# A Flamingo block on one core: the same steps of a hand-ordered pipeline in another order

## The chip, the cores and the metric

The kernel runs on one core of one Trainium2 chip. The metric is the device time of one execution in microseconds. Three runs of the kernel before gave 1331.11, 1333.94 and 1334.88 us; the median is 1333.94 us.

## The reference

The inputs are `x` (32 x 256 x 256, float32), a context `ctx_1024` (32 x 77 x 256), two gates and the weights. Cut to what matters:

```python
# cross attention, 8 heads of 128, no softmax over keys: everything is linear in the keys
f_q, f_k, f_v = proj(layernorm(x)), proj(ctx), proj(ctx)     # LN, then @ w_in.T, 8 heads
cosine_sim    = f_q @ f_k.T / (|f_q| |f_k|)
mixed         = cw*cosine_sim + vw*cosine_sim*decorr + ww*(q_ratio x k_ratio)   # weights per head
x = x + tanh(g_xattn) * ((mixed @ f_v) @ w_out.T + b_out)
# second attention, 16 heads of 16, softmax over 256 positions
z = layernorm(x); q, k, v = z@Wq, z@Wk, z@Wv
z = softmax(k q^T / 16, over the queries)^T @ v
z = gelu(l2norm(l2norm(z @ Wo) @ Wff))
x = x + tanh(g_ffn) * z
```

## The kernel before, in words

A setup phase (to about 170 us of the profile) computes statistics that need all of `x` and the whole context. Then `main_phase` works through 16 pairs of two batch rows each. The work on a pair is cut into some 260 named steps. Each step belongs to one engine and a few instructions:

- TensorE: `fk0..2` (keys of the heads), `G0..5` and `V0..5` (keys times the in- and out-projection), `zT0/1` and `zz0/1` (transposes), `q0..7` (queries, for their norms alone), `d0..5` (scores), `a0` (transpose of the query factors), `y0/1` (output of the first attention), `pq`, `pk`, `pv` (second attention's projections), `S0..15` (its scores), `P0..7` (probabilities times v), `O0..3` (output and the two l2 norms).
- ScalarE: a step with `.h` copies a bank of PSUM to its float16 high half; `X0..31` are the exponentials, `E0..3` copy the attended values, `O0.`..`O3.` take the squares, `F3` is the gelu, `pv0.v`, `a0.v` copy.
- VectorE: a step with `.l` subtracts the high half from the same bank and frees the bank; `M0..31` are the maxima of the scores, `R0..7` scale v, `d0.o`, `y0.o`, `q0.o` empty their banks, `z` normalises the rows of `x` for the next pair but one, `ln1/ln2` are the second layer norm, `qs1/qs2` the query factors, `F2/F4` the end of a pair.
- GpSimd: `rk`, `m0.l..m5.l`, `qpow`, `lpow`, `F1` (powers).
- SyncE issues every DMA: `ldx` (512 KB of `x` into `xin`, read by `z`), `aux`, `sqe0/sqe1` (12 broadcasts into `sqE`, read by `d0.o`, `d1.o`), `vt0/vt1` (DMA transposes, read by `y0`), `wq`, `ldy` (512 KB into `x2S`, read by `y0.o`), `res` (`x2S` to `x2`), `parts0/1` (queries and keys of the second attention to DRAM), `back0..3` (from there into `qstack` and `kstack`, read by `S0`, `S4`, `S8`, `S12`), `out`.

One list, `ORDER`, holds all steps. `run` lets each engine walk the list and execute its own steps, so the list fixes each engine's queue and nothing else; semaphores do the rest. A step never starts before its predecessor on its engine, and two steps of different engines are tied only by a semaphore. The list is software-pipelined: `lead(step)` says to which of three pairs in flight a step of one turn belongs (0, 1 or 2 turns back), and `MOVED` holds the exceptions. `HEAD` and `TAIL` are the shortened lists for the first and last two turns; 14 turns of `ORDER` lie between them.

All matmul steps but `S`, `P` share `WORK` = 3 banks of PSUM in the order of the list:

```python
CHUNKS = [s for s in ORDER if any(t.startswith(s + ".") for t in ORDER)]
A_INDEX = {name: k for k, name in enumerate(CHUNKS)}
...
def wait_free(eng, name, pair):
    eng.wait_ge(drained[A_INDEX[name] % WORK], uses(name, pair))
```

So a chunk can't start until the chunk three places before it in the list has been emptied (its `.l`, `.o` or `.v` step). There are 46 chunks, so at the turn of the list, where the last chunk and the first one both have bank 0, `a0` waits for the chunk right before it, `pv0`. Lines that the rows below name: L894 to L896 are the three products of every split matmul, L1388 `a0`, L1436 `S`, L1447 `P`, L1506 every `.h`, L1519 `pv.v`, L1533 `X`, L1557 `F3`, L1633 `a0.l`, L1684 `d.o`, L1693 `y.o`, L1730 `M`, L1602 `F1`, L1292 `parts`, L1302 `back`, L1245 `ldx`, L1250 `ldy`.

Of the kernel before, what the change touches and what calls it, by code (L numbers as in the profile page):

```python
# [974 lines left out]
TAIL = """
G4.h M2 a0 a0.v pv1 G4.l G5 a0.h M3 a0.l G0 aux X2 G5.h G5.l pv1.v G0.h S2 M4 V5 M5 G1 G0.l X3 G2 V5.h X4 res V5.l V2
S3 G1.h R0 back1 sqe0 G1.l G2.h V2.h M6 V4 V2.l M7 X5 S4 X6 M8 G2.l V4.h X7 M9 P0 X8 S5 V4.l d0 M10 X9 R1 M11 S6 X10
P1 sqe1 X11 d0.o d1 E0 M12 S7 vt0 M13 m0.h d1.o R2 d2 m0.l vt1 X12 X13 m1.h d2.o M14 M15 d3 m2.h d4 S8 wq m1.l X14 L0
m2.l ldy d3.o d4.o X15 P2 R3 m3.h d5 M16 m4.h X16 back3 S9 P3 M17 y0 M18 X17 m3.l S10 d5.o m5.h M19 X18 m4.l y0.o X19
M20 M21 X20 S11 X21 E1 m5.l M22 R4 M23 y1 L1 X22 S12 y1.o M24 P4 X23 M25 ln1 X24 R5 S13 O0 M26 O0. X25 M27 X26 S14 P5  # L980
lpow X27 M28 E2 S15 ln2 X28 M29 zz0 R6 L2 zz0.h zz1 zz1.h M30 zz0.l X29 zz1.l M31 X30 X31 O1 R7 P6 pq0 pq0.h pq0.l pk0
P7 pk0.h pk0.l E3 parts0 L3 O2 O1. O3 O2. pk1 O3. back0 F1 pq1 S0 pk1.h pk1.l pq1.h F2 pq1.l F3 M0 S1 back2 parts1 X0
M1 pv0 X1 pv0.v +back1 F4 +M2 out +M3 +S2 +X2 +M4 +pv1 +M5 +X3 +back3 +pv1.v +X4 +X5 +S3 +M6 +X6 +R0 +M7 +P0 +S4 +M8
+X7 +S5 +M9 +R1 +X8 +X9 +M10 +M11 +X10 +S6 +X11 +M12 +P1 +M13 +S7 +R2 +X12 +E0 +X13 +S8 +M14 +M15 +L0 +X14 +P2 +M16
+X15 +M17 +R3 +S9 +X16 +X17 +M18 +M19 +X18 +X19 +P3 +S10 +S11 +M20 +M21 +E1 +R4 +M22 +X20 +L1 +X21 +X22 +P4 +M23 +S12
+X23 +S13 +M24 +X24 +M25 +M26 +R5 +X25 +M27 +X26 +S14 +P5 +M28 +X27 +X28 +E2 +M29 +S15 +M30 +X29 +L2 +M31 +X30 +X31
+O0 +R6 +O0. +O1 +P6 +R7 +P7 +E3 +L3 +O2 +O1. +O3 +res +O2. +O3. +F1 +F2 +F3 +F4 +out
""".split()
# [815 lines left out]
```

## Time and profile before

| | |
|---|---|
| median of three runs | 1333.94 us (1331.11 to 1334.88) |
| the profiled execution | 1326.34 us, span 1324.6 us |
| mean granted TensorE clock | 0.978 of full |
| TensorE, VectorE, ScalarE, GpSimd busy | 1174.8, 1086.3, 1011.5, 299.3 us |
| DMA packets' share of 16 engines | 47.4% |

The profile is of one execution, 8 us shorter than the median of the runs. Busy time is the time in which an engine works on an instruction; where one engine is named behind an arrow, its instruction ended the idle time before the row's own. Times in rows are microseconds from the start of the span.

### The profile page before, as it was taken

What the parts mean: (1) busy time and instruction counts of PE and PEld (TensorE: products, weight loads), DVE (VectorE), ACT (ScalarE), POOL (GpSimd) and SP (SyncE); (2) the same over time, 40 slices, a digit from 0 to 9 for tenths busy, and PEclk for the clock granted to TensorE, in tenths of its full rate; (3) what the DMA queues carried; (4) which work ended last, traced back from release to release, by engine and by line L of the source; (5) the groups of instructions that cost most, each with busy time, mean ns of one, the idle gap of its engine ahead of it and who ended that gap; (6) DMA issues with size and microseconds to landing.
All of it is one profiled execution on the core that took longest, in us unless ns stands there. A gap on an engine that the chain in (4) does not pass through costs nothing.

```text
span 1324.6 us, 34636 instructions
## 1 busy us (share of the span) xinstructions
PE 1174.8 (89%) x10322; PEld 746.5 (56%) x10322; DVE 1086.3 (82%) x3084; ACT 1011.5 (76%) x3333; POOL 299.3 (23%) x257
## 2 busy tenths in 40 slices
...
GB/s 259 139 164 20 3 38 96 114 142 110 160 86 183 63 205 51 216 42 202 58 205 42 217 42 216 52 199 69 193 76 180 89 169 99 159 110 149 106 160 17
DMA packets 247888, 162.30 MB, mean 123 GB/s; under 512 B 94538, under 2 KB 235559, under 8 KB 247848
## 3 DMA queue, kind: packets, MB, share of 16 engines
q1 hardware_dynamic: 247848, 161.80, 47.4%
...
## 4 chain that ended last, share of the span: by engine, by line
PE 39%; SPq 22%; issue 9%; ACT 6%; DMA 5%; DVE 5%; POOL 1%; ACTq 0%; POOLq 0%; DVEq 0%; PEldq 0%
PE work L894 11%; PE work L896 10%; SPq L1281 10%; PE work L895 10%; PE attended L1447 5%; DMA x2S<-in_x 4%; SPq L1273 3%; SPq L1302 2%; SPq L1292 2%; PE score L1436 1%; ACT zb L1557 1%; SPq L1262 1%; ACT L1557 1%; PE work L1344 1%; ACT prob L1533 1%
## 5 line engine op out<-in xcount | busy, mean ns | idle before, releaser
L1533 ACT ACTIVATE prob<-score,nm 128x256 f32<-128x256 f32 x1024 | 477.1, 492 | 52.1 <-DVE nm L1730 46.2
L1730 DVE TENSOR_REDUCE nm<-score 128x2 f32<-128x512 f32 x512 | 332.6, 680 | 20.7 <-PE score L1436 20.2
L1533 ACT ACTIVATION_READ_ACCUMULATOR prob<-score,nm 128x1 f32 x1024 | 229.4, 224 | 0.0
L1590 POOL TENSOR_TENSOR mTl<-md,mTh 128x512 f16<-128x512 f32 (+1 forms) x96 | 95.2, 1006 | 378.0 <-ACT mTh L1506 378.0
L1447 PE MATMUL attended<-prob,vsp 128*32 128x256 f32 x2048 | 134.4, 391 | 9.7 <-DVE vsp L1745 8.4
L1436 PE MATMUL score<-qstack,kstack 64*128 64x256 f16 x1024 | 92.6, 277 | 40.9 <-DMA kstack<-parts 27.1
L1648 DVE BATCH_NORM_STATS2 qst<-work 128x6 f32<-128x128 f32 x512 | 110.4, 282 | 15.3 <-PE work L896 15.3
L1602 POOL TENSOR_TENSOR nrs<-nrm,phalf 128x8 f32<-128x8 f32 x16 | 26.3, 1642 | 355.8 <-ACT zb L1553 355.8
L894 PE MATMUL work<-wTh,xTh 128*128 128x512 f16 x256 | 98.3, 384 | 4.2 <-DVE xTl L1642 3.0
L895 PE MATMUL work<-wTl,xTh 128*128 128x512 f16 x256 | 97.7, 382 | 0.0
L896 PE MATMUL work<-wTh,xTl 128*128 128x512 f16 x256 | 97.6, 381 | 0.0
L1447 PEld LDWEIGHTS attended<-prob,vsp 128*32 128x32 f32 x2048 | 56.2, 110 | 68.5 <-issue 25.2
L894 PE MATMUL work<-Vph,mTh 128*128 128x256 f16 (+1 forms) x320 | 87.4, 273 | 7.7 <-DVE x2S L1693 4.1
L1593 POOL TENSOR_TENSOR rq<-qft,mhalf 128x32 f32<-128x32 f32 x16 | 86.8, 5428 | 29.7 <-DVEq L1657 29.7
L894 PE MATMUL work<-xTh,Gh 128*128 128x256 f16 (+1 forms) x320 | 87.6, 274 | 3.2 <-DVE fkl L1639 1.7
L1684 DVE SCALAR_TENSOR_TENSOR md<-work,rkc,sqE 128x256 f32<-128x256 f32 (+1 forms) x160 | 69.5, 476 | 23.7 <-DMA sqE<-sq_rows 15.3
L895 PE MATMUL work<-xTl,Gh 128*128 128x256 f16 (+1 forms) x320 | 87.2, 273 | 0.0
L896 PE MATMUL work<-xTh,Gl 128*128 128x256 f16 (+1 forms) x320 | 87.2, 273 | 0.0
L896 PE MATMUL work<-Vph,mTl 128*128 128x256 f16 (+1 forms) x320 | 87.1, 272 | 0.0
L895 PE MATMUL work<-Vpl,mTh 128*128 128x256 f16 (+1 forms) x320 | 87.0, 272 | 0.0
L1436 PEld LDWEIGHTS score<-qstack,kstack 64*128 64x128 f16 x1024 | 33.0, 94 | 93.1 <-issue 39.7
L1551 ACT ACTIVATE junk<-work 128x256 bf16<-128x256 f32 x128 | 48.4, 389 | 39.0 <-PE work L896 37.7
...
## 6 DMA issues: line engine op xcount, KB each, us to landing
...
xin<-in_x SPq DMA_DIRECT2D x16, 512.0 KB, 8.6
x2S<-in_x SPq DMA_DIRECT2D x16, 512.0 KB, 4.1
...
```

What stands on the lines that cost most here:

```text
L894: nc.tensor.matmul(out, a["h"][at], b["h"][bt], start=first, stop=False)
L895: nc.tensor.matmul(out, a["h"][at], b["l"][bt], start=False, stop=False)
L896: return nc.tensor.matmul(out, a["l"][at], b["h"][bt], start=False, stop=last)
L1281: sp.dma_start_transpose(Vp[half][:, :, :, o * P:(o + 1) * P].rearrange("p b t o -> p (b t) o"), VT[half][:, o, :, :].rearrange("p b c -> ...
L1436: last = nc.tensor.matmul(sc[2 * i + e][:, jj * NQ:(jj + 1) * NQ], kstack[rows, j, b2 * NQ + k * P:b2 * NQ + (k + 1) * P], qstack[rows, j, ...
L1447: last = nc.tensor.matmul(pvb[32 * j:32 * j + 32, t, :], vsp[:, k, (4 * e + j) * 2 * FD:(4 * e + j + 1) * 2 * FD], prob[:, n % PG, e, j, : ...
L1533: nc.scalar.activation(prob[:, g % PG, e, j + jj, :], sc[n % SC][:, jj * NQ:(jj + 1) * NQ], ACT.Exp, bias=nm[:, u + jj:u + jj + 1], accum_ ...
L1590: nc.gpsimd.tensor_tensor(dst, src, emptied(e[:2], "h")[0], ALU.subtract).then_inc(m_ready, 1)
L1593: nc.gpsimd.tensor_tensor(rq[:], qft[:, 0, :, :], w["mhalf"][:].rearrange("p (t h) -> p t h", h=H), ALU.pow).then_inc(rq_ready, 1)
L1648: last = nc.vector.bn_stats(qst[:, t, 4 * half + h, :], bank(e)[:, h * DH:(h + 1) * DH])
L1684: last = nc.vector.scalar_tensor_tensor(md[0:r, c % 2, k * 2 * P:(k + 1) * 2 * P], bank(e)[0:r, k * 2 * P:(k + 1) * 2 * P], rkc[0:r, t, b2 ...
L1730: nc.vector.tensor_reduce(nm[:, u:u + 2], sc[n % SC][:, :].rearrange("p (u q) -> p u q", q=NQ), AX.X, ALU.max, negate=True).then_inc(max_r ...
```

## The change

`ORDER`, `HEAD` and `TAIL` are replaced by other permutations of the same steps, and `MOVED` by another table of leads. No instruction is added, removed or resized, and no semaphore or buffer changes; the waits are computed from the lists, as before.

```diff
 ORDER = """
-G4.h M2 a0 a0.v pv1 M3 a0.h S2 pv1.v X2 G4.l a0.l G5 G0 V5 aux M4 res back1 G5.h G0.h G5.l sqe0 V5.h G0.l X3 G1 G2
-G1.h V5.l V2 G2.h R0 G1.l M5 S3 G2.l V2.h X4 M6 P0 V2.l M7 X5 V4 V4.h V4.l fk0 X6 fk0.h S4 M8 X7 fk0.l sqe1 M9 X8 R1
-fk1 d0 d0.o ldx fk1.h fk2 X9 fk1.l m0.h S5 S6 P1 M10 M11 vt0 d1 fk2.h X10 M12 X11 fk2.l X12 d1.o d2 S7 m0.l d2.o m1.h
-m1.l M13 m2.h d3 E0 M14 X13 vt1 M15 d4 d3.o R2 d5 X14 V1 S8 X15 m3.h L0 m2.l wq d4.o S9 R3 P2 M16 m3.l M17 M18 P3 m4.h
-X16 V1.h M19 X17 d5.o X18 E1 m4.l back3 m5.h ldy y0 z zT0 V1.l X19 L1 y0.o zT1 S10 S11 zT0.h M20 M21 M22 m5.l zT0.f
-zT0.l zT1.h X20 y1 zT1.f O0 X21 M23 X22 X23 R4 y1.o O1 O0. ln1 S12 O1. R5 S13 zT1.l P4 M24 P5 M25 M26 lpow ln2 E2 L2
-q0 q0.o X24 M27 q1 q1.o q2 X25 X26 q2.o q3 q3.o zz0 X27 S14 S15 q4 zz0.h zz0.l zz1 q5 zz1.h M28 q4.o X28 M29 zz1.l q6
-q5.o M30 X29 pq0 R6 pk0 M31 X30 q6.o X31 R7 P6 P7 pq0.h pq0.l pk0.h pk0.l parts0 E3 q7 L3 q7.o O2 O3 O2. V0 O3. V0.h
-qs1 V0.l pk1 pk1.h back0 F1 V3 pq1 F2 S0 pk1.l back2 V3.h F3 G3 pq1.h V3.l M0 G4 qpow pq1.l pv0 M1 F4 G3.h parts1 X0
-out qs2 pv0.v X1 S1 G3.l rk
+pv0.v X1 a0 G5 a0.v a0.h aux M3 G5.h G1 a0.l G1.h S2 rk X2 G5.l G2 pv1 M4 G2.h X3 pv1.v G1.l M5 X4 G2.l R0 V2 V2.h ldx
+X5 S3 fk0 M6 V5 fk0.h z V2.l P0 X6 S4 wq V5.h sqe0 M7 fk0.l M8 V5.l M9 d0 X7 X8 V4 R1 S5 X9 sqe1 fk1 M10 S6 d0.o V4.h
+P1 fk1.h X10 M11 V4.l E0 d1 fk1.l d2 m0.h L0 M12 M13 fk2 X11 vt0 m0.l X12 R2 X13 fk2.h d1.o S7 M14 M15 P2 d2.o S8 m1.h
+d3 X14 m1.l fk2.l X15 m2.h M16 V1 X16 d3.o R3 M17 d4 V1.h m3.h d5 S9 V1.l P3 X17 m2.l M18 S10 d4.o m3.l X18 E1 vt1
+d5.o m4.h res m5.h M19 L1 M20 X19 M21 zT0 back3 zT1 X20 R4 zT0.h y0 X21 zT0.f zT0.l m4.l P4 S11 zT1.h m5.l ldy M22 M23
+S12 y0.o zT1.f X22 zT1.l y1 O0 q0 M24 X23 y1.o R5 ln1 O0. S13 M25 X24 P5 X25 O1 M26 q1 O1. M27 lpow q0.o ln2 q2 X26
+q1.o E2 X27 q2.o q3 zz0 zz0.h q3.o S14 S15 zz1 q4 zz1.h M28 X28 zz0.l M29 zz1.l M30 X29 q4.o X30 q5 M31 pq0 pq0.h q6
+q5.o X31 L2 pk0 pq0.l R6 pk0.h R7 pq1 P6 P7 q6.o E3 q7 pk0.l pq1.h L3 O2 pq1.l O2. O3 q7.o pk1 parts0 back0 qs1 V0 O3.
+G4 pk1.h F1 pk1.l V3 F2 V0.h parts1 V0.l S0 G4.h F3 M0 qpow M1 G0 V3.h G4.l X0 V3.l S1 back2 F4 G3 qs2 back1 G0.h G3.h
+G0.l G3.l pv0 out M2
 """.split()
 
 HEAD = """
-ldx fk0 fk0.h fk0.l fk1 fk1.h fk1.l fk2 fk2.h fk2.l V1 z V1.h zT0 zT0.h V1.l zT1 zT0.f zT0.l zT1.h zT1.f zT1.l q0 rk
-q0.o q1 q1.o q2 q3 q2.o q4 q3.o q4.o q5 q5.o q6 q6.o G3 q7 V3 q7.o +ldx qs1 V0 V0.h V3.h qpow V3.l G4 V0.l qs2 G3.h
-G3.l +G4.h +a0 +a0.v +G4.l +a0.h +a0.l +G5 +G5.h +G0 +G0.h +G5.l +G1 +aux +wq +V5 +V5.h +G0.l +sqe0 +G1.h +G1.l +V5.l
...
+fk0 fk1 fk0.h fk1.h fk0.l fk1.l fk2 V1 ldx fk2.h z fk2.l V1.h V1.l zT0 zT0.h zT0.f zT0.l zT1 zT1.h zT1.f zT1.l q0 q0.o
+q1 q2 q1.o q2.o q3 q3.o q4 q4.o q5 q6 +ldx q5.o V0 q6.o q7 q7.o V0.h V3 qs1 G4 V0.l G4.h G0 G4.l G3 V3.h V3.l qpow
+G0.h G3.h G0.l G3.l +G1 qs2 +a0 +G5 +rk +a0.v +z +a0.h +G5.h +a0.l +G5.l +aux +V5 +G1.h +G2 +wq +G2.h +G2.l +G1.l +V2
...
 TAIL = """
...
-MOVED = {step: n for n, steps in {0: "G3 G3.h G3.l G4 V0 V0.h V0.l V1 V1.h V1.l V3 V3.h V3.l qpow qs1 qs2 rk", 1: "M0 M1 S0 S1 X0 X1", 2: "back1 back3 pv1 pv1.v res"}.items() for step in steps.split()}
+MOVED = {step: n for n, steps in {0: "G0 G0.h G0.l G3 G3.h G3.l G4 G4.h G4.l V0 V0.h V0.l V1 V1.h V1.l V3 V3.h V3.l qpow qs1 qs2", 1: "M0 M1 M2 S0 S1 X0", 2: "back3 pv0.v pv1 pv1.v res"}.items() for step in steps.split()}
```

## Rows read from the trace of the kernel before

**Rows 1.** Windows: 14 turns, one turn's front, its back; span, then busy us by engine

```profile
259.14:1217.07 957.93, 888.74 (x8345) 565.58 (x8345) 840.71 (x2269) 799.81 (x2703) 214.97 (x182) 1.00 0.51 129
602.31:653.72 51.41, 48.92 (x473) 32.40 (x474) 46.66 (x120) 43.78 (x159) 6.97 (x7) 1.00 0.55 125
653.72:670.99 17.27, 14.68 (x125) 7.97 (x124) 13.38 (x44) 13.38 (x36) 8.39 (x6) 1.00 0.46 144
```

**Rows 2.** Waits of the whole run: us in total, times, longest

```profile
PE score L1436 <- DMA kstack<-parts: 27.1, 18, 3.1
...
DVE md L1684 <- DMA sqE<-sq_rows: 15.3, 21, 1.8
...
PE work L1388 <- ACT v L1519: 10.6, 14, 1.0
```

**Rows 3.** Timeline of TensorE around one a0: start, us, instruction, idle before it

```profile
661.49 0.38 PE L894 MATMUL work<-zzTh,wkh 128*128 128x512 f16 x1
...
662.78 0.23 PE L894 MATMUL work<-fkh,woutTh 128*128 128x154 f16 x1
...
666.40 0.40 PE L1436 MATMUL score<-qstack,kstack 64*128 64x256 f16 x4 [1.54 <-DMA kstack<-parts]
666.73 0.24 PE L894 MATMUL work<-fkh,wNh 128*128 128x154 f16 x1
...
667.36 0.23 PE L894 MATMUL work<-fkh,wNh 128*128 128x154 f16 x1
...
670.99 0.66 PE L1388 MATMUL work<-ident,aux 128*128 128x128 f32 x4 [0.75 <-ACT v L1519]
...
674.18 0.24 PE L894 MATMUL work<-fkh,wNh 128*128 128x154 f16 x1 [0.38 <-DVE wqTl L1633]
```

**Rows 4.** Timeline of ScalarE before the same a0

```profile
662.98 0.60 ACT L1506 ACTIVATE kh<-work 128x512 f16<-128x512 f32 x1 [0.35 <-PE work L896]
...
664.18 1.28 ACT L1557 ACT_TABLE_LOAD   x1
665.47 1.70 ACT L1557 ACTIVATE zb<-zb,fac 128x256 f32<-128x256 f32 x4
...
668.13 1.28 ACT L1533 ACT_TABLE_LOAD   x1
669.43 0.47 ACT L1533 ACTIVATE prob<-score,nm 128x256 f32<-128x256 f32 x1
...
670.34 0.59 ACT L1519 ACTIVATE v<-work 128x512 f32<-128x512 f32 x1
```

**Rows 5.** Timeline of VectorE: four maxima in a row, and a0.l

```profile
626.96 2.47 DVE L1730 TENSOR_REDUCE nm<-score 128x2 f32<-128x512 f32 x4
...
673.37 0.68 DVE L1633 SCALAR_TENSOR_TENSOR wqTl<-work,wqTh 8x512 f16<-8x512 f32 x1 [0.40 <-ACT wqTh L1492]
```

**Rows 6.** Timeline of GpSimd: F1

```profile
662.26 1.64 POOL L1602 TENSOR_TENSOR nrs<-nrm,phalf 128x8 f32<-128x8 f32 x1 [21.08 <-ACT zb L1553]
```

**Rows 7.** SyncE's queue: parts0's and back0's first issue, out, aux

```profile
657.42 0.61 SPq L1292 DMA_DIRECT2D parts<-qh  x1
...
662.48 0.36 SPq L1302 DMA_DIRECT2D qstack<-parts  x1
...
671.36 1.13 SPq L1314 DMA_DIRECT2D out<-zb  x2
673.39 0.31 SPq L1256 DMA_DIRECT2D sq_rows<-sqT  x1
```

**Rows 8.** DMA issues by line, median us to landing; then ldx's least, median, longest

```profile
xin<-in_x SPq DMA_DIRECT2D x16, 512.0 KB, 8.6
x2S<-in_x SPq DMA_DIRECT2D x16, 512.0 KB, 4.1
...
DMA to landing us min/median/max: 4.3/8.6/9.4
```

**Rows 9.** Timeline of TensorE in the head: the first a0

```profile
202.14 1.08 PE L1388 MATMUL work<-ident,aux 128*128 128x128 f32 x4 [2.99 <-DVE aux L1668]
```

More of the change, by code:

```diff
@@ L966 @@
-q0.o q1 q1.o q2 q3 q2.o q4 q3.o q4.o q5 q5.o q6 q6.o G3 q7 V3 q7.o +ldx qs1 V0 V0.h V3.h qpow V3.l G4 V0.l qs2 G3.h
-G3.l +G4.h +a0 +a0.v +G4.l +a0.h +a0.l +G5 +G5.h +G0 +G0.h +G5.l +G1 +aux +wq +V5 +V5.h +G0.l +sqe0 +G1.h +G1.l +V5.l
-+G2 +G2.h +V2 +G2.l +V4 +V2.h +V4.h +V2.l +fk0 +V4.l +fk0.h +fk0.l +fk1 +sqe1 +vt0 +fk1.h +d0 +d0.o +fk2 +fk1.l +d1
-+fk2.h +d2 +z +m0.h +fk2.l +vt1 +m0.l +d1.o +d3 +d2.o +m1.h +m1.l +m2.h +d3.o +m2.l +d4 +m3.h +m3.l +d5 +d4.o +m4.h
-+V1 +d5.o +m4.l +V1.h +y0 +m5.h +zT0 +zT0.h +zT0.f +ldy +m5.l +V1.l +zT1 +y0.o +y1 +zT1.h +zT0.l +zT1.f +zT1.l +y1.o
@@ L971 @@
-+q0 +ln1 +lpow +q1 +q0.o +q1.o +ln2 +q2 +q3 +q2.o +q3.o +zz0 +q4 +zz0.h +zz0.l +q4.o +zz1 +q5 +zz1.h +zz1.l +q6 +q5.o
-+q6.o +pq0 +pq0.h +pk0 +pq0.l +q7 +pk0.h +pk0.l +pk1 +q7.o +V0 +pk1.h +V0.h +pk1.l +V3 +V0.l +pq1 +V3.h +pq1.h +qs1
-+G3 +parts0 +pq1.l +pv0 +back0 +qpow +rk +V3.l +S0 +M0 +G3.h +pv0.v +X0 +S1 +M1 +X1 +parts1 +G3.l +back2 +G4 +qs2
+fk0 fk1 fk0.h fk1.h fk0.l fk1.l fk2 V1 ldx fk2.h z fk2.l V1.h V1.l zT0 zT0.h zT0.f zT0.l zT1 zT1.h zT1.f zT1.l q0 q0.o
+q1 q2 q1.o q2.o q3 q3.o q4 q4.o q5 q6 +ldx q5.o V0 q6.o q7 q7.o V0.h V3 qs1 G4 V0.l G4.h G0 G4.l G3 V3.h V3.l qpow
@@ new lines @@
+G0.h G3.h G0.l G3.l +G1 qs2 +a0 +G5 +rk +a0.v +z +a0.h +G5.h +a0.l +G5.l +aux +V5 +G1.h +G2 +wq +G2.h +G2.l +G1.l +V2
++V2.h +sqe0 +sqe1 +fk0 +V2.l +d0 +fk0.h +fk0.l +V5.h +V4 +d0.o +V5.l +V4.h +fk1 +fk1.h +m0.h +V4.l +fk1.l +d1 +fk2
++d1.o +m1.h +d2 +m0.l +vt0 +d3 +vt1 +d2.o +m2.h +m1.l +m2.l +fk2.h +V1 +fk2.l +d3.o +d4 +ldy +V1.h +d5 +V1.l +d4.o
++m3.h +m4.h +zT0 +zT0.h +m3.l +m4.l +zT1 +zT0.f +zT1.h +d5.o +zT0.l +y0 +m5.h +m5.l +zT1.f +zT1.l +y0.o +y1 +q0 +q1
++y1.o +ln1 +lpow +q0.o +q1.o +q2 +ln2 +q3 +q2.o +q3.o +zz0 +zz0.h +zz1 +zz0.l +zz1.h +q4 +zz1.l +q5 +q4.o +q5.o +pq0
@@ L974 @@
++q6 +pq0.h +pk0 +pk0.h +pq0.l +pq1 +pq1.h +q6.o +pk0.l +q7 +pq1.l +q7.o +parts0 +G4 +pk1 +pk1.h +qs1 +V0 +V0.h +G4.h
++V0.l +pk1.l +G0 +V3 +V3.h +qpow +G4.l +V3.l +G3 +G0.h +G3.h +back0 +S0 +G0.l +parts1 +M0 +back2 +G3.l +qs2 +M1 +pv0
++back1 +S1 +M2 +X0
 """.split()
 TAIL = """
-G4.h M2 a0 a0.v pv1 G4.l G5 a0.h M3 a0.l G0 aux X2 G5.h G5.l pv1.v G0.h S2 M4 V5 M5 G1 G0.l X3 G2 V5.h X4 res V5.l V2
-S3 G1.h R0 back1 sqe0 G1.l G2.h V2.h M6 V4 V2.l M7 X5 S4 X6 M8 G2.l V4.h X7 M9 P0 X8 S5 V4.l d0 M10 X9 R1 M11 S6 X10
@@ L978 @@
[L978 to L987, printed above, removed]
+pv0.v a0 X1 G1 G5 a0.v S2 a0.h M3 a0.l X2 G5.h aux G5.l res X3 M4 G1.h X4 M5 G2 G1.l pv1 S3 sqe0 X5 V2 M6 S4 G2.h
@@ new lines @@
+pv1.v V2.h M7 V5 R0 M8 X6 V5.h P0 G2.l M9 V5.l sqe1 X7 V4 V2.l S5 rk X8 R1 X9 d0 M10 V4.h S6 X10 M11 d0.o X11 m0.h M12
+P1 X12 V4.l S7 d1 M13 R2 d2 E0 M14 L0 X13 X14 M15 S8 d1.o X15 m1.h wq m0.l M16 m1.l d2.o P2 M17 d3 S9 R3 X16 X17 d3.o
+d4 vt0 M18 P3 M19 m2.h vt1 m3.h m2.l d5 d4.o X18 X19 S10 S11 m3.l E1 m4.h d5.o M20 M21 M22 X20 m4.l ldy M23 m5.h m5.l
+X21 back3 y0 S12 L1 y1 R4 M24 X22 X23 M25 y0.o O0 P4 R5 y1.o S13 ln1 lpow M26 O0. M27 P5 X24 X25 X26 X27 S14 ln2 E2
+M28 M29 zz0 zz1 zz0.h zz1.h X28 X29 S15 zz0.l zz1.l M30 O1 L2 pq0 M31 pk0 X30 X31 pq0.h R6 R7 pk0.h P6 P7 E3 pq0.l pq1
```

6 lines of the change are left out of this document (added).

## The prediction, made before the changed kernel was run

> **What bounds the kernel now.** I read the windows first, for the 14 turns of `ORDER` between the first `a0` of turn 1 and that of turn 15 [rows 1]. They take 957.93 us, so 68.42 us a turn, of which TensorE works 63.5, VectorE 60.0 and ScalarE 57.1. Nothing but order can be won here: TensorE idles 4.9 us a turn. The window of one turn splits them: 2.5 us in the front (`a0` to `pk0`, 51.41 long, 48.92 busy), 2.6 in the back (`pk0` to the next `a0`, 17.27 long, 14.68 busy). VectorE is close behind, so a stall of it is often one of TensorE a step or two later.
>
> Then the table of waits [rows 2]. Transfers end 27.1 us of TensorE's waits at `S`, 15.3 us of VectorE's at `d.o`: 42.4 us in all, 3 us a turn. If all of that were on the path, its removal would be worth some 40 us, and this is what the list's new distances could give.
>
> The timelines tell whether it is on the path. In the back, `S0` waits 1.54 us for `kstack`, and the next `a0` still waits 0.75 us, for the copy `pv0.v` of ScalarE [rows 3]. ScalarE's own timeline up to that copy is almost solid [rows 4]: `pk1.h` at 662.98 starts when `pk1` is done, then `V3.h`, a load of the gelu table (1.28 us), the gelu (1.70), `pq1.h`, `G3.h`, a load of the exp table (1.28), `X0`, `pv0.v`, `a0` at 670.99. From the end of `pk1` to `a0` are 8.0 us, and `S0`'s wait lies wholly beside them: `X0` needs `M0`, which needs `S0` (666.40), but ScalarE reaches `X0` after its load, at 669.43. So in the back the transfer is a wait that is seen, not the one that decides; the chain from `pk1` over four copies, gelu, two table loads, `X0` and `pv0.v` to `a0` is.
>
> **The change, part by part.** No step gets cheaper. I lay the new list along the measured durations, an engine's next step starting at the later of its own queue and the step that releases it.
>
> *Back.* Origin: start of `pk0`. Before, `pk0` started at 653.72 [rows 1] and the copy of `pk1` 9.26 us after it [rows 4]. `pq1` is now put before `pk1`, and `V0` behind it. A step of six products of 512 columns takes 1.3 us (`pk1` at 661.49 to `V3` at 662.78), one like `V0` 0.63 (`G3` at 666.73 to `G4` at 667.36) [rows 3]. So `pk1` is done at 9.26 + 1.30 - 0.63 = 9.93. ScalarE's queue is now `pk1.h V0.h G4.h` load, gelu, `V3.h` load, `X0 G0.h G3.h pv0.v`: six copies instead of four beside the same gelu, loads, `X0` and `pv0.v`. Two copies take 1.20 us up to the first load and 0.96 from the gelu's end (667.17) to the second [rows 4], so one costs 0.5 to 0.6 and the chain is 8.0 + 1.1 = 9.1; in detail: copies at 9.94, 10.5, 11.2 (`G4` ends at 11.14), load 11.8, gelu 13.05, `V3.h` 14.7, load 15.25, `X0` 16.55 (0.91 to `pv0.v` [rows 4]), `G0.h` 17.5, `G3.h` 17.95, `pv0.v` 18.45, done at 19.0. `pv0` is now the last chunk right before `a0`, with the same bank, so `a0` starts at 19.05 instead of 17.27: +1.8 us. The stretch holds one chunk more (`G0`, 0.6 us of TensorE, moved here from the front), so 1.2 us of it are new idle time.
>
> VectorE doesn't bind there, but is near: `F1` (1.64 us on GpSimd [rows 6]) now starts at about 9.8, when `O3.` is done; `F2` runs 11.4 to 12.65, and `V0.l` behind it frees `G0`'s bank at 13.3, where `G0` could have gone at 12.5. `S0` has its turn at about 12. `back0` starts 5.1 us after `parts0`'s first issue [rows 7], and `S0` could start 3.9 after that (666.40 [rows 3]); `parts0` starts at 3.2, behind `pk0.l`, so `back0` at 8.3 and it lands by 12.2. The 1.5 us wait of `S0` thus all but vanishes, and is worth nothing: it is paid again at `G0`, `G3` and `a0`.
>
> *Front.* Origin: `a0`. It has 0.6 us of work less. Of its 2.5 us of idle time before, 0.38 is the bank after `a0`, behind `a0.l` [rows 3, 5]; the rest (2.1) comes mostly behind VectorE, which is held at `d0.o` and `d1.o` by `sqE` for 0.7 us each time [rows 2]. In the new list:
> - ScalarE: `X1` to 0.85, `a0.v` 1.4, `a0.h` 1.95; VectorE `a0.l` to 2.65 (it had idled 0.8). Between `a0` and `G2`, whose bank is `a0`'s, lie only `G5`, `G1`, `S2`, to 2.0: `G2` waits 0.8 us. Before, `pv1` (1.4 us) filled most of this.
> - SyncE: `aux` was issued 2.4 us after `a0` [rows 3, 7]; with `out` and `back1` done before it, 2.1; with a pause of 0.3 us, `ldx` behind it at 2.65, no longer behind 12 broadcasts. A quiet 512 KB load lands in 4.1 us, the one behind the broadcasts in 8.6 [rows 8]. I take the quiet one, as the queue ahead (`out`, `aux`) is over by then: xin is there at 6.8. `z`, for which VectorE had its turn long after the landing, now has VectorE's turn at about 6.65 (`M2 M3 a0.l G5.l M4 G1.l M5 G2.l R0 M6` before it: a maximum 0.60 us, 2.47 for four [rows 5], a `.l` about as much, `a0.l` done at 2.65). So the stall is 0.15 us. This is the one place where the distance shrinks. The bank of `d0` is freed by `V2.l`, right behind `z`, at 8.8: `d0` starts at 8.9.
> - `sqe0` is issued at 5.3, with `res` and `back1` no longer in its way, and the rows bound its landing by the quiet load's 4.1 and the crowded one's 8.6 [rows 8]: 9.4 to 13.9. I take 12.5, nearer to the crowded, as it is five transfers behind `ldx`; `d0.o` comes at 12.8. `sqe1` is issued from 7.1, for `d1.o` at 17.4, and is there even by 9.4. So both waits go: 15.3 us in 14 turns, 1.1 a turn [rows 2]; at the late bound `d0.o` keeps 1.1, and TensorE 0.8 of it at `d1`, +11 us in all.
> - VectorE stays about 1 us behind TensorE to `y0`: waits of 0.3 (`d1`), 0.3 (`P2`), 0.4 (`zT1`, on `d4.o`), 0.1 (`y1`).
> - `vt1` lands near 23 against `y0` at 26; `wq` is long there; `ldy` now waits for `res` and lands near 30, against `y0.o` at 32.7.
>
> Sum of the front: 0.8 + 0.05 + 0.3 + 0.3 + 0.4 + 0.1 = 1.95 us of waits for 2.5 before, so it is 0.6 + 0.55 = 1.15 us shorter. A turn: +1.8 - 1.15 = +0.65; in 14 turns +9.
>
> *Head and tail.* The head's first `a0` waits 2.99 us for the chain over GpSimd's powers [rows 9]; `G0` and `G1` now stand before it and fill 1.2 of it. The tail I leave at zero. Together 9 - 1 = +8 us on the profiled execution's 1326.3, 1334; on the median, 8 us higher, 1342.
>
> For the landing of `ldx` the Trainium skill ("DMA: Bandwidth & Descriptors", the section on the anatomy of one DMA) has a fit of 2.0 us and 436 KB for each further microsecond. By it, an estimate, 512 KB land in 3.2 us, the stall of `z` is nil and the sum 2 us lower; the rows have 4.1 for `ldy` and never under 4.3 for `ldx` [rows 8], so it is a floor here.
>
> **The rivals.**
> - *The transfers' waits decide after all, and it is faster.* For it: VectorE's release from `sqE`, 1.1 us a turn, comes where TensorE hangs on VectorE. If only the 0.8 us at `G2` are left in the front, it is 2.3 us shorter, the turn 1.8 - 2.3 = -0.5, so -7 - 1 = -8: 1326; with a back chain 0.5 shorter (copies that slip in while ScalarE waits) another -7: 1319. It decides when the front's idle time falls under 1.3 us a turn. Against it: VectorE works 60 us of a turn [rows 1], and in the new list loses 2.3 us at `L3`, 1 at `pk1.l`, 0.8 at `a0.l`, which it can't make up ahead of `d0`.
> - *`ldx` lands late.* If the queue is still busy, its landing is 8.6 and `z` stalls 4.6 us, every turn, with `V2.l` and `d0` behind it: +4.5 x 14 = 63 us on my case, 1405. At 5.5 us it would be 1.2 a turn more, +17 on my case: 1359. For it: `back1` and `out` now come last before it, 1 MB. Against it: `out`'s issue ends near `a0`, 2.6 us earlier.
> - *An even trade.* The front gains what the back loses (1.3 us of waits left in the front, 0.65 fewer): 1334 within 4.
>
> **How the numbers follow.** What a measurement here can tell from no change is about 0.3%, 4 us. My case, 0.5 to 1.1 us a turn, 1338 to 1350: 0.43. Faster: 0.29. Even: 0.17. `ldx` late or another wait that the laying-out misses: 0.11. The order is laid out by hand over 260 steps, and an error of 1 us a turn is 14 us, so the range takes in the faster rival (1319) and a late landing of 5.5: 1318 to 1360. Faster 0.30, same 0.18, slower 0.52.
>
> **What would show it.** The period between two `a0` at 69.0 to 69.2 instead of 68.42. `pk0` to `a0` at 19 instead of 17.3, with `pv0.v` ending it and TensorE idle before `G0`, `G3`, `a0`. No waits on `kstack` or `sqE` of note; `G2` waiting 0.8 for `a0.l`; `ldx` landing in 4 to 4.5. I am wrong if `pk0` to `a0` is under 18, if `z` waits over 0.5 us for `xin`, or if TensorE's idle time between `a0` and `pk0` is far from 2 us.

## The result: 0.75% faster

The changed kernel takes 1324.26 us (median of four runs, 1322.42 to 1325.61), the kernel before, beside it on the same chip, 1334.41 (1331.11 to 1336.44): ratio 0.9925, interval 0.9901 to 0.9949. The prediction had 1342 and called slower the likelier; the time lies in its range, the direction was wrong.

The profiled execution of after takes 1325.61 us, span 1323.9. Its windows, as in [rows 1]: the 14 turns from `a0` to `a0`, then one turn's front and its back (span, then busy us of TensorE, its weight loads, VectorE, ScalarE, GpSimd; granted clock, DMA share, GB/s).

```profile
263.99:1219.28 955.29, 896.57 (x8344) 565.83 (x8345) 820.97 (x2268) 798.60 (x2703) 207.04 (x182) 1.00 0.49 131
674.12:723.30 49.18, 48.34 (x463) 31.71 (x464) 44.82 (x118) 43.96 (x162) 6.95 (x7) 1.00 0.45 113
723.30:742.27 18.97, 15.73 (x135) 8.70 (x133) 13.87 (x46) 13.08 (x34) 7.83 (x6) 1.00 0.57 176
```

The front runs from `a0` to `pk0`, the back from `pk0` to the next `a0`. The back is 1.7 us longer than in [rows 1], the front 2.2 shorter. TensorE's idle time in the front fell from 2.5 us to 0.84, that in the back rose from 2.6 to 3.24. From turn 2 on every front is 49.18 to 49.20 us long. Before, they were 50.2 to 52.0.

The table of waits of the whole run (us, times, longest):

```profile
PE work L1389 <- ACT v L1520: 22.3, 15, 1.6
...
PE work L894 <- DVE Gl L1640: 12.1, 17, 1.6
...
PE work L894 <- DVE wqTl L1634: 10.0, 15, 0.7
...
PE score L1437 <- DMA kstack<-parts: 5.4, 3, 3.6
```

Against [rows 2]: VectorE has no row of `sqE` any more, and TensorE's row of `kstack` falls from 27.1 us to 5.4. The wait of `a0` for `pv0.v` has doubled. What is left in TensorE's back, as in [rows 3]: `V3`, `G0`, `G3`, `a0`, and then `G2` in the next front.

```profile
734.63 0.24 PE L894 MATMUL work<-fkh,woutTh 128*128 128x154 f16 x1 [0.18 <-DVE kl L1640]
...
736.69 0.24 PE L894 MATMUL work<-fkh,wNh 128*128 128x154 f16 x1 [0.81 <-DVE VTl L1640]
...
738.42 0.24 PE L894 MATMUL work<-fkh,wNh 128*128 128x154 f16 x1 [0.62 <-DVE Gl L1640]
...
742.27 0.66 PE L1389 MATMUL work<-ident,aux 128*128 128x128 f32 x4 [1.55 <-ACT v L1520]
...
744.93 0.24 PE L894 MATMUL work<-fkh,wNh 128*128 128x154 f16 x1 [0.66 <-DVE wqTl L1634]
```

ScalarE's timeline up to the same `a0`, as in [rows 4]: copy of `pk1`, `V0.h`, `G4.h`, load, gelu, `V3.h`, load, `X0`, `G0.h` with `G3.h`, `pv0.v`.

```profile
733.25 0.60 ACT L1507 ACTIVATE kh<-work 128x512 f16<-128x512 f32 x1 [0.18 <-PE work L896]
733.87 0.56 ACT L1507 ACTIVATE VTh<-work 128x462 f16<-128x462 f32 x1
734.48 0.56 ACT L1507 ACTIVATE Gh<-work 128x462 f16<-128x462 f32 x1
735.06 1.28 ACT L1558 ACT_TABLE_LOAD   x1
736.35 1.71 ACT L1558 ACTIVATE zb<-zb,fac 128x256 f32<-128x256 f32 x4
737.96 0.54 ACT L1507 ACTIVATE VTh<-work 128x462 f16<-128x462 f32 x1
738.52 1.28 ACT L1534 ACT_TABLE_LOAD   x1
739.81 0.47 ACT L1534 ACTIVATE prob<-score,nm 128x256 f32<-128x256 f32 x1
...
740.73 1.00 ACT L1507 ACTIVATE Gh<-work 128x462 f16<-128x462 f32 x2
741.60 0.61 ACT L1520 ACTIVATE v<-work 128x512 f32<-128x512 f32 x1
```

From `pk1`'s copy to `pv0.v` ScalarE stops for nobody. From `pk0` (723.30) the steps stand at 9.95, 10.57, 11.18, 11.76, 13.05, 14.66, 15.22, 16.51, 17.43 and 18.30.

The transfers: `ldx` and `ldy` both land in 3.6 us at the median, where [rows 8] has medians of 8.6 and 4.1; `ldx` lands in 3.4 at the least.

When the transfers land and when their readers start, in us after `a0`, least / median / longest of turns 2 to 14 (worked out from each trace by step):

| | front | `sqe0` lands | `d0.o` | `sqe1` lands | `d1.o` | `ldy` lands | `y0.o` |
|---|---|---|---|---|---|---|---|
| before | 50.2/51.2/52.0 | 12.1/12.8/14.0 | 13.15 (median) | 16.6/17.5/18.6 | 17.50 | 29.1/30.1/30.9 | 30.07 |
| after | 49.2/49.2/49.2 | 10.7/11.1/12.0 | 12.22 | 14.6/15.1/15.6 | 16.87 | 25.8/26.4/26.8 | 31.48 |

In before the median turn has `d1.o` and `y0.o` 0.02 us behind the landing that they need, so the turn follows the landings and their scatter of 2 us. The wait that ends last is the one at `y0.o`: in 27 of the 28 turns of before's two profiles (the second is below) `y0.o` starts 0.02 us behind the landing of `ldy`, and `pk0` follows 21.10 us after it, whatever `d0.o` and `d1.o` waited. Its row in the table of waits of before is small:

```profile
DVE x2S L1693 <- DMA x2S<-in_x: 6.2, 13, 1.0
```

SyncE's queue tells why `ldy` is late. This is before, in the turn that starts at 670.99: `ldx`, the two transposes of `vt0`, then `ldy`, and VectorE's `y0.o`.

```profile
681.11 0.41 SPq L1245 DMA_DIRECT2D xin<-in_x  x1
682.05 5.66 SPq L1281 DMA_TRANSPOSE Vph<-VTh  x1
687.86 2.62 SPq L1281 DMA_TRANSPOSE Vpl<-VTl  x1
...
697.30 0.38 SPq L1250 DMA_DIRECT2D x2S<-in_x  x1
```

```profile
701.47 0.69 DVE L1693 SCALAR_TENSOR_TENSOR x2S<-work,x2S 128x512 f32<-128x512 f32 x1 [0.57 <-DMA x2S<-in_x]
```

`ldx` lands 9.16 us after its issue, at 690.27, and the issue of the second transpose ends at 690.48. It is so in 27 of the 28 turns: that issue ends 0.16 to 0.22 us after `ldx` has landed, and `ldy` is issued 6.8 to 7.1 us after the same landing. So before's turn hangs on `ldx`, by way of the transposes' place in the queue and of `ldy`. The chain of work that ended last, by engine, says the same (first before, then after; SPq is SyncE's queue): in before it runs through the landing of `ldy` in 12 of the 14 turns (13 in the second profile), in after through no landing from turn 2 on.

```profile
PE 39%; SPq 22%; issue 9%; ACT 6%; DMA 5%; DVE 5%; POOL 1%; ACTq 0%; POOLq 0%; DVEq 0%; PEldq 0%
PE 66%; ACT 10%; issue 6%; DVE 3%; DMA 1%; ACTq 0%; SPq 0%; POOL 0%; POOLq 0%; PEldq 0%; DVEq 0%
```

In after `ldx` comes long ahead of the transposes. From turn 2 on each reader has a margin of 0.2 us at the worst landing (`d0.o`) to 4.6 us (`y0.o`), and nothing scatters.

### The profile page after: what moved, and what is told of

It reads as the page before. It is cut to its first block, busy times and chain, and to the rows that moved or that the text cites. A ratio compares the mean times of both kernels' runs of the same rounds, so it can differ in the third digit from the quotient of the medians.

```text
span 1323.9 us, 34712 instructions
## 1 busy us (share of the span) xinstructions
PE 1186.1 (90%) x10322; PEld 748.6 (57%) x10322; DVE 1066.7 (81%) x3084; ACT 1008.6 (76%) x3333; POOL 291.5 (22%) x257
## 4 chain that ended last, share of the span: by engine, by line
PE 66%; ACT 10%; issue 6%; DVE 3%; DMA 1%; ACTq 0%; SPq 0%; POOL 0%; POOLq 0%; PEldq 0%; DVEq 0%
PE work L894 18%; PE work L896 16%; PE work L895 16%; PE attended L1448 8%; PE score L1437 4%; ACT prob L1534 3%; PE work L1345 2%; ACT L1534 1%; ACT L1558 1%; ACT Gh L1507 1%; ACT zb L1558 1%; DVE wqTl L1634 1%; ACT wqTh L1493 1%; ACT VTh L1507 1%; ACT v L1520 1%
## 5 line engine op out<-in xcount | busy, mean ns | idle before, releaser
L1534 ACT ACTIVATE prob<-score,nm 128x256 f32<-128x256 f32 x1024 | 481.4, 495 | 18.6 <-DVE nm L1731 14.7
L1731 DVE TENSOR_REDUCE nm<-score 128x2 f32<-128x512 f32 x512 | 336.8, 680 | 9.3 <-PE score L1437 9.0
L1534 ACT ACTIVATION_READ_ACCUMULATOR prob<-score,nm 128x1 f32 x1024 | 232.7, 227 | 0.0
L1448 PE MATMUL attended<-prob,vsp 128*32 128x256 f32 x2048 | 137.4, 392 | 1.9 <-DVE vsp L1746 1.0
L1437 PE MATMUL score<-qstack,kstack 64*128 64x256 f16 x1024 | 97.5, 279 | 18.7 <-ACT prob L1534 13.0
L894 PE MATMUL work<-fkh,wNh 128*128 128x154 f16 x256 | 56.1, 238 | 35.0 <-DVE VTl L1640 14.4
```

Source lines behind the costliest of these rows:

```text
L894: nc.tensor.matmul(out, a["h"][at], b["h"][bt], start=first, stop=False)
L1437: last = nc.tensor.matmul(sc[2 * i + e][:, jj * NQ:(jj + 1) * NQ], kstack[rows, j, b2 * NQ + k * P:b2 * NQ + (k + 1) * P], qstack[rows, j, ...
L1448: last = nc.tensor.matmul(pvb[32 * j:32 * j + 32, t, :], vsp[:, k, (4 * e + j) * 2 * FD:(4 * e + j + 1) * 2 * FD], prob[:, n % PG, e, j, : ...
L1534: nc.scalar.activation(prob[:, g % PG, e, j + jj, :], sc[n % SC][:, jj * NQ:(jj + 1) * NQ], ACT.Exp, bias=nm[:, u + jj:u + jj + 1], accum_ ...
L1731: nc.vector.tensor_reduce(nm[:, u:u + 2], sc[n % SC][:, :].rearrange("p (u q) -> p u q", q=NQ), AX.X, ALU.max, negate=True).then_inc(max_r ...
```

## The experiments

Two theories stood at first. A: before hangs on the landings of `sqE` (and `ldy`) in each front, after doesn't, and that is the gain. B: the new order of the compute steps is the gain. The ratio is always to the kernel before on the same chip. All diffs are of the lists alone, if nothing else is said. The text of A on record names `kstack` beside `sqE`; that wait turned out to be free ("The back", below).

### Both kernels again

No edit.

> The kernel before once more, unchanged. Theory A (before hangs on the landings of sqE and kstack in each turn, so their spread enters its time; after hangs on none): ratio to itself 1.00 within 0.3%, and its profiled turns from a0 to a0 differ from one another by up to 2 us (67.5 to 69.3), with each d0.o starting within 1.6 us behind the landing it waits for. Theory B (the gain lies in the order of the compute steps, not in transfers): the same ratio, but the turns' lengths don't follow the landings.

> The kernel after once more, unchanged. Both theories: ratio 0.990 to 0.996. Theory A alone: profiled turns all 68.14 us within 0.1, since no transfer ends a wait of TensorE, VectorE or ScalarE in the front, and time without the profiler within 2 us of the profiled one.

Ratios 0.9996 (0.9979 to 1.0012) and 0.9928 (0.9905 to 0.9951); medians 1334.12 and 1324.08 us. The 14 turns of this execution of before, and its waits for transfers:

```profile
260.72:1227.47 966.75, 890.62 (x8344) 566.54 (x8344) 840.19 (x2269) 800.61 (x2703) 214.86 (x182) 1.00 0.51 128
```

```profile
DVE md L1684 <- DMA sqE<-sq_rows: 20.6, 24, 2.1
...
DVE x2S L1693 <- DMA x2S<-in_x: 8.9, 13, 1.1
```

They took 966.75 us where the first profile had 957.93 [rows 1]: the same kernel, 8.8 us apart in 14 turns. The first of the 14 is 72.3 us long, 3.5 more than in the first profile, and the granted clock fell in it, to 0.51 in a stretch of its front. The profile that the prediction was made from was a lucky one (1326.34 us; this one 1339.9; all of before's runs here lie between 1326.3 and 1343.0). After's turns in its second profile are 68.13 or 68.14 us in 11 of 14, but the first is 68.8, 0.7 more than A said. All runs of after lie between 1322.4 and 1327.5. So far A, but the landing that counts is that of `ldy`.

### The queues exchanged

`old_steps_new_queue`: before's compute queues, after's SyncE queue. `new_steps_old_queue`: the reverse, `ldx` alone left behind `aux`. The SyncE steps of one turn:

```diff
 # old_steps_new_queue
-aux res back1 sqe0 sqe1 ldx vt0 vt1 wq back3 ldy parts0 back0 back2 parts1 out
+aux ldx wq sqe0 sqe1 vt0 vt1 res back3 ldy parts0 back0 parts1 back2 back1 out
 # new_steps_old_queue
-aux ldx wq sqe0 sqe1 vt0 vt1 res back3 ldy parts0 back0 parts1 back2 back1 out
+aux ldx res back1 sqe0 sqe1 vt0 vt1 wq back3 ldy parts0 back0 back2 parts1 out
```

> The kernel before with SyncE's steps in after's order and at after's distances (ldx right behind aux, then wq, sqe0, sqe1; res after vt1; back1 last before the turn of the list); every compute engine keeps before's queue. Theory A: sqe0 lands near 12 instead of 13 and sqe1 near 15 instead of 17.5 us after a0, d0.o and d1.o stop waiting, the front falls from 51.2 to 50.1, the back stays 17.25: 67.4 us a turn, 1.0 less than before, in all 14 us less, ratio 0.985 to 0.992. Theory B: the front keeps within 0.3 us of before's and the ratio is 0.997 to 1.003.

> The kernel after with SyncE's steps in before's order (ldx alone stays behind aux, as z reads it early): res and back1 ahead of sqe0, sqe0 and sqe1 later, ldy behind back3. Theory A: sqe0 lands at 14 or later where d0.o has its turn at 12.2, so the front grows by 1 to 2 us and the turn is 69 to 70 instead of 68.14: ratio to before 1.003 to 1.02. Theory B (after's compute order is what gains): as after, ratio 0.990 to 0.996, front within 0.3 us of 49.2.

1.0195 (1.017 to 1.0219) and 1.0199 (1.0168 to 1.023): each half alone is 2% slower than before. The second was slower as A said, but by another transfer, and by more than it said. `back1` now lands at 10 us where `S4` has its turn at 8.3, so `S4` waits 1.6 to 2.4 us, `d0.o` comes later by about as much, and `sqE` ends only 2.3 us of waits in the whole run. The front is thus 50.8 to 51.3 us long in eight turns. In the other six it is 52.4 to 53.0, and these are the six in which the granted clock fell right behind `S4`'s wait. Here is the stretch behind `S4`'s wait in two neighbouring turns: one of 70.14 us, where `S4` waited 2.0 us, and one of 71.38, where it waited 1.8 (span, then busy us; the last three columns are granted clock, DMA share, GB/s):

```profile
484.30:487.30 3.00, 3.00 (x38) 2.44 (x35) 2.52 (x6) 2.02 (x9) 0.00 (x0) 1.00 1.81 232
...
554.30:557.30 3.00, 3.00 (x18) 2.33 (x18) 2.07 (x5) 1.93 (x8) 0.00 (x0) 0.51 1.55 240
```

The first missed under both theories, though its first turn was the 67.5 us of A. From its second turn on `sqe0` is issued at 9.7 instead of 6.2. TensorE's `a0`, and SyncE's queue around it (the first issue of `parts1`, the last of `back2`, the first of `back1`, then `out`, `aux`, `ldx` and `sqe0`):

```profile
682.98 0.66 PE L1389 MATMUL work<-ident,aux 128*128 128x128 f32 x4 [0.73 <-ACT v L1520]
```

```profile
680.62 0.52 SPq L1293 DMA_DIRECT2D parts<-qh  x1
...
683.68 0.78 SPq L1303 DMA_DIRECT2D kstack<-parts  x1
686.00 0.36 SPq L1303 DMA_DIRECT2D qstack<-parts  x1
...
687.26 1.12 SPq L1315 DMA_DIRECT2D out<-zb  x2
689.28 0.31 SPq L1257 DMA_DIRECT2D sq_rows<-sqT  x1
689.86 0.41 SPq L1246 DMA_DIRECT2D xin<-in_x  x1
...
692.63 4.65 SPq L1274 DMA_DIRECT2D sqE<-sq_rows  x12
```

`back1` reads what `parts1` writes. In after's queue it comes right behind it and has to wait until `parts1` has landed (5.4 us from `parts1`'s first issue to `back1`'s), and `out`, `aux`, `ldx` and `sqe0` stand behind it. `parts1` needs the copy of `pq1`, which before's order makes behind the gelu, 2.4 us ahead of `a0`. VectorE then waits 47.7 us for `sqE` (13 times, longest 4.4). That is not all of the loss: in nine of the turns the granted clock fell as well, around the end of a pause of TensorE of 2.2 to 3.2 us behind VectorE's wait, and these are 70.7 to 71.9 us long, the turns 2 to 14 without it 69.7 to 70.5. In after `pq1` comes ahead of `pk1`, and `parts1` is issued 7.5 us ahead of `a0`. So that move pays for a queue.

### The link tested: `pq1` alone

`old_steps_new_queue` with `pq1` one place earlier and its copies ahead of the gelu (in the head `V0` also goes ahead of `V3`, whose bank it now shares):

```diff
-V0 O3. V0.h qs1 V0.l pk1 pk1.h parts1 F1 V3 pq1 F2 S0 pk1.l back2 V3.h F3 G3 pq1.h V3.l M0 G4 qpow pq1.l pv0
+V0 O3. V0.h qs1 V0.l pk1 pk1.h parts1 F1 pq1 pq1.h V3 F2 S0 pk1.l pq1.l back2 F3 V3.h G3 M0 V3.l G4 qpow pv0
```

> The kernel before with after's SyncE queue, as in old_steps_new_queue, and in addition the chunk pq1 with its copies moved from behind V3 and the gelu to right behind pk1, ahead of V3 and the gelu. Theory: old_steps_new_queue lost because back1, now ahead of the turn's end, waits for parts1 to land, and parts1 is issued only 2.4 us before a0 when pq1.l comes behind the gelu; aux, ldx, sqe0 and sqe1 all queue behind it. With pq1 early, parts1 is issued near 5 us before a0, sqe0 near 6 us after a0 instead of 9.7, and lands near 13; the back is 0.6 us longer (one more copy between pk1 and the gelu), 17.85, the front 50.3 to 51: turn 68.1 to 68.9 instead of 70.8, ratio 0.988 to 1.00. Rival (the slower time of that run came from something else, such as contention of back1 with the front's transfers): ratio still near 1.02.

0.9963 (0.9938 to 0.9988) instead of 1.0195; back 17.93 us, 17.85 laid out. `sqe0` is issued at 7.0 and lands at 12.5 to 13.1 in ten of the turns 2 to 14, which are 68.1 to 68.4 us long; where it lands at 13.65 to 14.15, the turn is 68.8 to 69.3. The rival is out, and the granted clock falls in none of the turns.

### One transfer moved, and four

```diff
 # before_res_later: SyncE's steps of a turn
-aux res back1 sqe0 sqe1 ldx vt0 vt1 wq back3 ldy ...
+aux back1 sqe0 sqe1 ldx vt0 vt1 res wq back3 ldy ...
 # transfers_only
+aux back1 sqe0 sqe1 vt0 vt1 ldx res wq back3 ldy ...
```

> The kernel before with one step of SyncE moved: res, which stands ahead of back1 and sqe0, goes behind vt1, as in after. sqe0 is then issued 0.9 us earlier (4.6 instead of 5.5 us after a0). Theory A (before hangs on the landings of sqE): sqe0 lands at 12.0 to 12.8 and sqe1 near 16.7, d0.o and d1.o lose most of their 0.8 us and 0.6 us of waits, the front falls from 51.5 to 50.6 to 50.9 us and the ratio is 0.988 to 0.993: one moved transfer gives what the whole change gives. Theory B (the waits are not on the path, or the landing doesn't follow the issue): front within 0.3 us of 51.5, ratio 0.997 to 1.003.

> The kernel before with every compute engine's queue as it is, and four steps of SyncE's moved: res and ldx from ahead of vt0 to behind vt1, wq after them, back3 and ldy last as before (aux back1 sqe0 sqe1 vt0 vt1 ldx res wq back3 ldy). Theory (the change's gain is in its transfers, its compute steps cost): sqe0 lands at 11 to 12.5, sqe1 before 16.7, ldy before 28.9 us after a0, no landing ends a wait in the front, which is 50.2, the back 17.25: 67.45 a turn, every turn alike, 14 turns in 944 us, ratio 0.983 to 0.988, faster than the change itself. Rival (after's order of the compute steps is needed for the gain): the front stays above 51 and the ratio is 0.993 or more.

`before_res_later`: 0.9966 (0.9947 to 0.9985), front 51.1 us, between the two expectations. `sqe0` lands at 11.8, `sqe1` at 16.25, and VectorE's waits for `sqE` go, but its waits for `x2S` (`y0.o` on `ldy`) rise from 6.2 and 8.9 us in the two profiles of before to 13.3: `ldy` still lands at 30.0 and `y0.o` starts at 30.05, where it could go at 28.95. `res` now stands behind `vt1`, so `ldy` is issued 8.0 us after `ldx`'s landing instead of 7.0, which takes back what the earlier `ldx` gave. So the waits for `sqE`, taken away alone, are worth next to nothing: they were not the last (the chain that ended last goes through the landing of `ldy` in all 14 turns here). Where `ldy` isn't late they do count, as the turns of `pq1_early_new_queue` with a late `sqe0` show.

`transfers_only` (the tail's `res` is moved too): 1317.55 us, 0.9867 (0.984 to 0.9894), with every compute queue as before. Faster than after, whose interval in the same way is 0.9905 to 0.9951. Its 14 turns, and its waits for transfers in the main phase of VectorE and TensorE:

```profile
257.35:1202.85 945.50, 887.78 (x8344) 565.30 (x8344) 841.77 (x2269) 797.97 (x2703) 215.05 (x182) 1.00 0.50 131
```

```profile
DVE x2S L1693 <- DMA x2S<-in_x: 0.2, 1, 0.2
...
PE score L1436 <- DMA kstack<-parts: 26.4, 16, 2.9
```

67.54 us a turn, front 50.20. `sqe0` lands at 10.5 to 12.1 (reader 13.14), `sqe1` at 14.2 to 15.6 (reader 16.92), `ldy` by 29.2 (reader 28.94). With `ldx` behind the transposes, the second one's issue ends 0.2 to 0.3 us after `sqe1` has landed, and `y0.o` starts at 28.94 instead of 30.07. B is out: the whole gain and more is to be had without one compute step moved. Four transfers were moved at once; that `ldx` alone would do is read from the queue and not shown by a run. After's 68.24 are 0.7 a turn more (front and back 49.18 + 18.96 against 50.16 + 17.25 in turns where no landing ends a wait in the front), so its compute order costs 10 us in 14 turns.

### An extra transfer

Before and after with 256 KB copied from DRAM to DRAM ahead of `sqe0`, its landing awaited only at the end:

```diff
+sp.dma_start(spare[bass.ds(a * NQ, NQ), :], x_rows[bass.ds(a * NQ, NQ), :]).then_inc(spare_in, 16)
```

> The kernel before with an extra transfer of 256 KB from DRAM to DRAM in each turn, issued right before sqe0, whose landing nothing waits for until the end. Theory (before's turn follows the landings of sqE): sqe0 and sqe1 land 0.5 to 2 us later, and the turn grows by as much: ratio 1.007 to 1.03. Rival (it doesn't hang on them): ratio under 1.003.

> The kernel after with the same extra transfer at the same place. sqe0 lands at 10.8 to 12.0 with its reader at 12.2 us, sqe1 at 15 with its reader at 16.9. Theory (after has margin): a landing 1 us later costs 0 to 0.8 us a turn at d0.o, less than it costs before: ratio to before 0.992 to 1.004. Rival (both are limited alike): as much as before, ratio 0.999 to 1.02.

1.0097 (1.0064 to 1.013) and 0.9991 (0.9968 to 1.0014): 13 us more on before, 9 more on after. VectorE's waits for `sqE` go from 20.6 us to 29.9 in before, from none to 7.9 (9 times, longest 1.5) in after. The order is A's, but the intervals of the two costs overlap, so this pair doesn't decide. What it shows is that after's margin of a median 1.1 us at `d0.o` is spent by 256 KB: it is small. In before `pk0` still follows `y0.o` by 21.10 us in every turn, and `y0.o` the landing of `ldy` by 0.02. The clock fell in two turns of each, so a part of both costs is not the landings'.

### The back

`pv0v_first` is after with ScalarE's `pv0.v` ahead of `G3.h` (in the tail too). In the other two, after and `transfers_only`, the gelu is left out (`ACT.Gelu` becomes `ACT.Copy`, with the same scale), so ScalarE loads no tables there; each of these two was run twice.

> The kernel after with one copy of ScalarE moved: pv0.v ahead of G3.h, at the end of the back. If ScalarE's chain from pk1 to pv0.v sets a0, as the prediction says, the back falls from 18.96 by one copy less what pv0 itself allows, 0.3 to 0.5 us, and G3.h, G3.l and with them the bank of G1 come 0.5 us later, so the front grows by 0 to 0.5: turn 67.8 to 68.2, ratio to before 0.987 to 0.993. If the chain doesn't set a0, the back keeps 18.96.

> The kernel after with the gelu of the second attention replaced by a scaled copy, so ScalarE loads no table of functions between pk1 and a0 (this leaves out the gelu). If ScalarE's chain sets the back, the copies' start is then held by F2 (12.7 us after pk0), X0 comes 1.6 us earlier and a0 with it: back 17.2 to 17.6 instead of 18.96, and the turn 1 to 1.7 us shorter, ratio to before 0.97 to 0.98. If the turn's length is VectorE's or TensorE's, the front takes it back and the turn is less than 0.5 us shorter.

> The kernel transfers_only with the gelu replaced by a scaled copy, so ScalarE loads no tables between pk1 and a0 (this leaves out the gelu). There S0 waits 1.5 us for kstack in every turn. Theory (that wait lies beside ScalarE's chain and costs nothing; the chain from pk1 to pv0.v sets a0): without the second load X0 starts at about 14.4 instead of 15.7 us after pk0, pv0 ends at 16.2, and a0 comes at 16.8 instead of 17.25, though S0 waits as long as before. Rival (S0's wait sets the back): the back stays at 17.2 to 17.3.

`pv0v_first`: back 18.52 instead of 18.96, front 49.72 instead of 49.18, turn 68.23. TensorE's `a0` and `G2`:

```profile
741.75 0.66 PE L1389 MATMUL work<-ident,aux 128*128 128x128 f32 x4 [1.11 <-ACT v L1520]
...
744.86 0.24 PE L894 MATMUL work<-fkh,wNh 128*128 128x154 f16 x1 [0.79 <-DVE wqTl L1634]
```

`pv0.v` sets `a0`, as predicted, but the gain is given back behind it: ScalarE has `G3.h`, `X1` and `a0.v` to do before `a0.h` in either order, and `G2` waits for `a0.h` by way of `a0.l`. The ratio was 1.0 (0.9981 to 1.0018) all the same, 10 us slower than after, of which the 14 turns show 2; the tail, where the copy was moved too, is 7.6 us longer (112.1 against 104.6 from the last `a0` to the end).

`after_no_gelu`: 0.9864 (0.9818 to 0.9909); back 17.9 to 18.0 in 11 turns, 1 us less, not the 1.4 to 1.8 expected, and the median turn 67.53 instead of 68.14. ScalarE's chain set the back, but right behind it lies VectorE's: `F1`, `F2`, `V0.l`, `G4.l`, and `G3` still waits 0.62 us for it. `transfers_no_gelu`: 0.9852 (0.9823 to 0.988); back 16.77 on the mean, the 16.8 laid out, with `S0` waiting as long as ever (below). The front gives 0.2 us back, the 14 turns are 0.3 us shorter each, and the two ratios can't be told apart.

```profile
727.89 0.39 PE L1436 MATMUL score<-qstack,kstack 64*128 64x256 f16 x4 [1.53 <-DMA kstack<-parts]
...
731.92 0.66 PE L1388 MATMUL work<-ident,aux 128*128 128x128 f32 x4 [0.44 <-ACT v L1519]
```

So in before the longest row of transfers' waits of TensorE, 27.1 us of `kstack` [rows 2], lay beside ScalarE's chain and cost nothing; VectorE's 15.3 us for `sqE` were not the last wait either; the smallest of the three, its 6.2 us for `x2S`, was the one that counted.

## Why the prediction was wrong

It fell by two terms of its sum, both of which laid the changed kernel out too slow and so turned the direction, and by what it took for the limiter of the front. It held in most other steps.

- *The back* was right: 19.05 us laid out, 18.97 measured, and each copy within 0.15 us (laid out at 9.94, 10.5, 11.2, 11.8, 13.05, 14.7, 15.25, 16.55, 17.5, 18.45). That `S0`'s wait is worth nothing was right, shown by `transfers_no_gelu`.
- *The front* is the first term that failed: "VectorE stays about 1 us behind TensorE to `y0`", 0.3 + 0.3 + 0.4 + 0.1 = 1.1 us of waits. Of the four only 0.07, at `P2`, came. Of 1.95 us laid out 0.84 were left: `G2` 0.66 (0.8 laid out), `pv1` 0.11, `P2` 0.07. VectorE was a little earlier than laid out at every point, and the error grew along the queue:

```profile
680.52 0.16 DVE L1624 COPY st<-stats 128x8 f32 x1
680.81 1.38 DVE L1628 TENSOR_SCALAR norm<-xin,st 128x256 f32<-128x256 f32 x4
...
686.35 0.86 DVE L1685 SCALAR_TENSOR_TENSOR md<-work,rkc,sqE 128x256 f32<-128x256 f32 x2
```

  With `a0` at 674.12, `z` starts at 6.40 (6.65 laid out), `d0.o` at 12.23 (12.8), `d1.o` at 16.87 (17.4) and `y0.o` at 31.48 (32.7). 0.6 us in 20 steps turn waits of 0.3 into none. A turn was thus to be 69.07 us and is 68.24 on the mean, 955.3 in 14 instead of 967: 11.7 us.
- *The limiter of before's front.* The prediction gave the 2.1 us of idle time there to VectorE, held at `d0.o` and `d1.o` by `sqE`. The wait that ended last, in 25 of the 28 turns of the two profiles by the chain, was that of `y0.o` for `ldy`, which the prediction doesn't count, and what made `ldy` late was `ldx` ahead of the transposes. That the front's waits would go with the new queue was right, by another transfer than the one named; the removal of `sqE`'s waits alone left `y0.o` at 30.05 us (`before_res_later`).
- *The step from the profile to the median* is the second, 9.3 us. I took the profile's distance to the median, 8 us, as a constant and added it to after. It was before's own scatter: 966.75 us of turns in its second profile, 957.93 in the first, 3.5 of the 8.8 us in the one turn in which the clock fell, the rest with the landings. A kernel that waits for no landing doesn't have it; after's median lies 1.3 us below its profile.
- *Head and tail* were to give -1: the turns begin 4.9 us later (263.99 against 259.14; 2.4 later if the second profiles are compared), and the tail is 3.0 shorter, +1.9 in all, 2.9 more than the -1. The sum 1342 - 11.7 - 9.3 + 2.9 = 1324 is the time measured.
- *The transfers.* `ldx` "quiet" was right: 3.6 us at the median (4.1 taken), and `z` doesn't wait for it. The Trainium skill's fit ("DMA: Bandwidth & Descriptors", anatomy of one DMA), which the page gives for transfers that GpSimd issues and the prediction applied to one of SyncE, puts 512 KB at an estimated 3.2 us. This trace has nothing under 3.4. `sqe0` lands at 11.1 (12.5 taken), `ldy` at 26.4, not 30. That both waits of `sqE` go was right.
- *The rival that came true* is "the transfers' waits decide after all", 1326 us, with its condition met (under 1.3 us idle in the front: 0.84). It had 0.29. What spoke against it, VectorE's lost time in the back, was there as described and did not reach `d0`. Its mechanism was another transfer's wait than it named (`ldy`, not `sqE`), and larger than I made it: 68.42 or 69.05 us a turn in the two profiles of before against 67.54 with the transfers moved alone, so the landings cost before 0.9 to 1.5 us a turn (the larger figure includes the turn with the fallen clock). Of that the compute order gives back 0.7.

Left open: why the clock fell in some turns of `new_steps_old_queue` and not in others, whether `ldx` moved by itself gives the whole gain, and how much of after's compute order is needed beyond `pq1` to carry its queue.
